# Moving one copy of the rotary query split from VectorE to ScalarE, at 14 places of an attention kernel

## What is computed

```python
q_C = (c_Q @ W_UQ.T)            # 16 heads, 128 wide
q_R = rope(c_Q @ W_QR.T, pos)   # 16 heads, 64 wide: the rotary queries
q = concatenate([q_C, q_R]); k = concatenate([k_C, rope(x @ W_KR.T, pos)])
scores = clip(einsum('bhqd,bhkd->bhqk', q, k), -80, 80)
weights = softmax(where(causal, scores, -inf) / sqrt(192))
attn = einsum('bhqk,bhkd->bhqd', weights, v)
out = x + (attn @ W_O.T) * silu(ffn(x))
```

## Time and profile before

| what | us |
|---|---|
| median of 3 runs | 1460.11 |
| lowest, highest | 1458.19, 1461.9 |
| the profiled execution's own time | 1460.29 |
| its span, first to last instruction | 1458.8 |
| TensorE busy | 1383.0 |
| VectorE busy | 1155.1 |
| ScalarE busy | 769.5 |
| GpSimd busy | 111.4 |

### The profile page before, as it was taken

One profiled execution on the slowest core, in us unless ns is written; L12 is line 12 of the kernel. 1 busy time (PEld: TensorE's weight loads), 2 busy tenths in 40 slices (PEclk: granted clock), 3 DMA queues, 4 the chain that ended last, 5 costly groups with the idle time before them and its releaser, 6 DMA issues. The chain is left out here.

```text
span 1458.8 us, 27828 instructions
## 1 busy us (share of the span) xinstructions
PE 1383.0 (95%) x9808; PEld 1120.5 (77%) x9808; DVE 1155.1 (79%) x1336; ACT 769.5 (53%) x840; POOL 111.4 (8%) x150
## 2 busy tenths in 40 slices
PE   4999689999999999999999999999999899599998
PEld 4888567777778888887878888887888788278887
DVE  4666388898898898989888898899788699476664
ACT  3322356656665656565666656656656566332221
POOL 0000111101001000000010000000100000112121
PEclk9999899999999999999999999999999999899999
DMA  6423565545425424333142421421422511345652
GB/s 253 144 73 101 161 201 160 164 136 145 126 84 153 116 93 99 109 101 108 54 147 62 126 83 54 126 83 54 131 58 61 217 57 58 117 125 158 183 171 87
DMA packets 111949, 172.77 MB, mean 118 GB/s; under 512 B 9224, under 2 KB 68904, under 8 KB 109096
## 3 DMA queue, kind: packets, MB, share of 16 engines
q1 hardware_dynamic: 97528, 111.10, 24.7%
q0 software_dynamic: 13552, 59.60, 14.0%
q10 hardware_dynamic: 832, 1.57, 0.5%
HBM read 123.75 MB, written 48.50 MB: 118 GB/s over the span
## 5 line engine op out<-in xcount | busy, mean ns | idle before, releaser
L1093 ACT CAST prob_h<-prob 128x1024 fp32r<-128x1024 f32 (+1 forms) x288 | 289.8, 1006 | 245.8 <-DVE prob L1174 195.7
L1087 ACT ACTIVATE prob<-score_ps 128x1024 f32<-128x1024 f32 (+1 forms) x288 | 281.9, 979 | 170.5 <-PE score_ps L946 117.2
L1192 DVE TENSOR_TENSOR prob_l<-prob,prob_h 128x1024 fp32r<-128x1024 f32 (+1 forms) x288 | 336.0, 1167 | 39.7 <-ACT prob_h L1093 38.3
L946 PE MATMUL score_ps<-q_h,key_slot 64*128 64x512 f32 x1792 | 357.8, 393 | 7.9 <-DMA key_slot<-keys 7.8
L968 PE MATMUL out_ps<-prob_h,value_slot 64*128 64x512 f32 (+1 forms) x1792 | 340.4, 377 | 5.5 <-DVE prob_l L1192 5.0
L1187 DVE TENSOR_TENSOR total<-total,prob 128x1024 f32<-128x1024 f32 (+1 forms) x256 | 294.9, 1152 | 0.0
L1174 DVE TENSOR_SCALAR prob<-prob 128x1024 f32<-128x1024 f32 x224 | 155.1, 692 | 80.3 <-ACT prob L1087 80.1
L946 PEld LDWEIGHTS score_ps<-q_h,key_slot 64*128 64x128 f32 x1792 | 170.9, 185 | 48.2 <-DMA key_slot<-keys 7.3
L968 PEld LDWEIGHTS out_ps<-prob_h,value_slot 64*128 64x128 f32 x1792 | 170.7, 185 | 48.1 <-DVE prob_l L1192 12.2
L946 PE MATMUL score_ps<-q_l,key_slot 64*128 64x512 f32 x896 | 177.7, 391 | 0.0
L946 PE MATMUL score_ps<-rot_hh,key_slot 64*128 64x512 f32 x896 | 177.5, 390 | 0.0
(11 more groups left out here) (192 smaller groups left out, 1975.5 us busy)
## 6 DMA issues: line engine op xcount, KB each, us to landing
key_slot<-keys SPq DMA_DIRECT2D x144, 256.0 KB, 2.7
value_slot<-values SPq DMA_DIRECT2D x144, 128.0 KB, 2.0
rows<-heads_rows SPq DMA_DIRECT2D x32, 512.0 KB, 5.7
rot_hh<-turned POOLq DMA_DIRECT2D x30, 512.0 KB, 6.2
heads_rows<-head_rows POOLq DMA_DIRECT2D x15, 1024.0 KB, 9.5
turned<-rot_hl POOLq DMA_DIRECT2D x14, 1024.0 KB, 5.1
rot_l<-turned POOLq DMA_DIRECT2D x30, 256.0 KB, 7.6
wo<-in_w_o POOLq DMA_DIRECT2D x1, 4096.0 KB, 13.3
```

The source lines that it names most:

```text
L946: mm = pe.matmul(score_ps[:, half, c * 512:(c + 1) * 512], keys_of[ROWS[r], :], moving[par][ROWS[r], half * HW + c * 512:half * HW + (c + ...
L1087: nc.scalar.activation(prob[half][:, 0:width], score_ps[:, half, 0:width], ACT.Exp, scale=QK_SCALE).then_inc(exp_done, 1)
L1093: nc.scalar.copy(prob_h[half][:, 0:width], prob[half][:, 0:width]).then_inc(high_done, 1)
L1192: nc.vector.tensor_tensor(p_l, p, p_h, ALU.subtract).then_inc(split, 1)
```

## The change

In the program of ScalarE, behind its second `high` of a LATE pair of couple 0 and of a FULL pair k = 1 of the other couples, stands a copy of `rot_f` into the high half of `rot_hl`, with the waits that VectorE's copy had. VectorE keeps only the difference.

```diff
@@ ScalarE: def pair(t, unit, k, slot, kind, prev) @@
                     for half in range(2):
                         exponential(half)
                         high(half)
+                    first_couple = isinstance(unit.couple, int) and unit.couple == 0
+                    if unit.has_second and (kind == LATE and first_couple or
+                                            kind == FULL and isinstance(k, int) and k == 1):
+                        since(act, passed, 16 * n)
+                        act.wait_ge(r_step, 4 * n + 2)
+                        nc.scalar.copy(rot_hl[:, 0, :, :], rot_f[:, :, :]).then_inc(r_step, 1)
                     return
@@ VectorE: def split_turned(n) @@
-                since(dve, passed, 16 * n)
-                dve.wait_ge(r_step, 4 * n + 2)
-                nc.vector.tensor_copy(rot_hl[:, 0, :, :], rot_f[:, :, :]).then_inc(r_step, 1)
                 dve.wait_ge(r_step, 4 * n + 3)
                 nc.vector.tensor_tensor(rot_hl[:, 1, :, :], rot_f[:, :, :], rot_hl[:, 0, :, :],
                                         ALU.subtract).then_inc(r_step, 1)
```

## The result

| | us |
|---|---|
| before, median of 11 runs | 1458.69 |
| changed, median of 11 runs | 1453.53 |
| lowest and highest, before / changed | 1457.36, 1461.9 / 1449.74, 1456.6 |
| ratio, with its 95% interval | 0.9956 [0.9947, 0.9965] |
| span of the profiled execution, before / changed | 1458.8 / 1452.1 |

A forecast was written before the change was run, and what follows sets the result against it. TensorE was taken to set the time, stalled ten times by VectorE's copy and difference. -7.15 (units 4 to 13) - 0.9 (units 2 and 3) + 0.65 (units 0 and 1) = -7.4 us, giving 1452.7 us; range 1450.5 to 1457.5.

The forecast's parts named there:

- What bounds the kernel: TensorE sets the time; ten waits for `prob_l` behind VectorE's copy and difference in units 4 to 13 lose 7.6 us.
- The size of the stalls: Units 4 to 13: each place gets back the smaller of its loss and 0.72 us, 7.15 us in all.
- the bracket of idle time (0.45): Listed idle time at a TensorE stall, counted from the modelled end of the matmul before; distances of starts gave 0.71 lost.
- The cover on ScalarE: At the 12 FULL places the copy costs nothing: 0.2 us ahead of need, next exponential 0.4 us or more to spare.
- Couple 0: Units 0 and 1: nothing covers the copy, the difference starts 0.35 and 0.3 us later; cost +0.65 us, bounds 0.3 and 2.1.
- Couple 1: Units 2 and 3: TensorE's stalls for `total` and the turned products at the next CORNER end; 0.9 us gained, bounds 0.4 and 1.2.
- Rival 1: Another wait, a later `prob_l` or a key tile, comes due at the ten places; half of each stall stays: 1456.8, chance 0.12.
- Rival 2: ScalarE's copy starts late and is hidden nowhere; 0.35 us at each of 14 places, +4.9 us: 1465.0, chance 0.05.
- The rule against the change: Skill advice to use VectorE, not ScalarE, for simple elementwise work; by it alone the copy's move would give the slower 1465.0.

## Why the prediction was right, and where not

**What bounds the kernel: right.** The ten waits for `prob_l` were one event, they belong to the block of copy and difference on VectorE, and they are gone. Lengthening the block by 0.60 us lengthened each stall by 0.60.

**The size of the stalls: right.** 7.15 us were forecast for couples 2 to 6, and units 4 to 13 are 7.0 us shorter. That the bracket of idle time (0.45) is not the loss (0.71), and that the starts have to be compared, made the difference between 5.0 and 7.15. It could be checked so closely because units 5 to 13 repeat to 0.1 us between profiles of the kernel before.

**The cover on ScalarE: right.** The copy was worked out to start 0.95 us behind the high half and the exponential 1.90; they do (516.60, 517.55, 518.50). The clip came 0.72 us earlier against its low half, as said. The 0.4 us to spare were 0.45.

**Couple 0: the local delay is right, its price in time is not shown.** +0.35 and +0.3 were forecast, and the difference starts 0.35 and 0.33 us later in both kernels that have this part. What it costs disappears in the scatter of loads and of the clock: unit 0 takes 25.7 to 26.35 us where VectorE does the copy and 26.0 to 26.7 where ScalarE does, unit 1 differs by 1.6 us between profiles of before, and units 0 and 1 together came out at +1.3 in the change instead of +0.65.

**Couple 1: the gain is there, in one of its two stalls.** -0.9 was forecast for what follows units 2 and 3, and these take 1.4 us less in the mean, more than forecast. TensorE's summing matmul behind unit 2 came 0.56, 1.01 and 1.02 us behind the matmul ahead of it in the profiles of before (0.56 is the one in the earlier trace rows) and comes at 0.32 in all four of the change; behind unit 3 it is 0.51, 0.48 and 0.47 against 0.32 to 0.34. The stall for the turned products did not end at unit 3's CORNER as forecast: 0.56 us before, 0.48 to 0.58 after. Waits for key tiles of 1.0 and 1.4 us stand in units 2 and 3 in the change's first profile and of 0.6 and 1.1 in that of before, so the size is not a clean number.

**The step that was missing**: the key tile behind the load of `wo`. Rival 1 named key tiles, but at the ten places, where no wait for one is listed in any of these profiles. In the rest of units 4 to 13 its waits for them add up to 1.5 to 2.3 us in the profiles of before and to 1.6 to 4.8 in those of the change, and yet these units are 7.0 us shorter. The loss came at the end: +1.9 us in units 14 and 15, which the forecast took as moving rigidly with the rest. So `attend` is 5.3 us shorter in the profiles and not 7.4. The timed runs say 6.0 to 6.7 in four comparisons. The profiles come near to that only with the 1.0 us that stands ahead of `attend`; whether the timed runs hold such a part too isn't shown, and if they do, the total agrees better than the forecast earned. Why that key tile comes later in the kernels with both parts stays open.

**Rival 2's price** does not follow from its own condition. It says that the gain ends when the copy is 0.92 us late (0.72 + 0.2; its 0.95 is a slip) and then charges 0.35 at every place. With the second copy on ScalarE it is about that late, and the clip starts 3.04 us behind the low half instead of 3.00 before: 0.04 a place, and the time of before, not 1465.

**The rule against the change** (the Trainium skill, ScalarE: Activation LUTs, Rules for kernel authors) names `relu`, `max`, `min`, `add` and `mul` as work for VectorE; to apply it to a copy, as the prediction did, goes one step further. The trace agrees on the instruction, 1.05 us against 0.69. As a decision it would have been wrong at the ten places, where VectorE was waited for and ScalarE was not. In couple 0, where nothing covered the copy, its price is what the trace shows: the difference starts 0.35 us later.

## What to carry to other kernels

Look for the one stall that repeats with a period of the program, and count it: ten waits for ten units said more than an engine at 79%. Measure it by the starts of the waiting engine's instructions, and price the cover of the engine that takes the work by two numbers, how long until its result is needed and how long until its next instruction is; here 0.2 and 0.45 us, so that one copy was free and a second took all the gain back. Where the gain is a few us, compare the stretches that repeat between profiles to a tenth, and not the whole time, which moves by two us and more by itself (1457.36 to 1461.9 for the kernel before).

## What the runs showed of the hardware

- A matmul stream that resumes after a stall for its operand loses about 0.10 us more than the gap: the next start is 0.34 us behind instead of 0.23 (528.43 and 528.77; at all ten stalls of the three profiles of before, and not here in the change, 523.16 and 523.39). The same 0.34 stands at a few of the ten places in the change, where TensorE starts 0.05 to 0.06 us behind the end of `prob_l` and no wait is listed.
- Two casts on ScalarE, 1.05 us each, start 0.95 us apart; two on VectorE, 0.69 each, start 0.60 apart where the second waits for nothing (527.59 and 528.19); VectorE's difference, which waits for the copy, starts 0.72 behind it (523.48 and 524.20).
- The wait for a 256 KB key tile behind a 4 MB load differs by kernel (4.3 to 5.0 us in eight profiles, 5.7 to 6.4 in six) and repeats within each to 0.7 us, although the two loads are issued at the same distance. What decides it stays open.
- At the same place of the program, after a wait of 1.9 to 3.1 us for a gather, TensorE's clock was at 1.2 GHz in some executions and at 2.4 GHz in others of the same kernel (0.51 in one of before, 1.00 in two), which goes with about 2 us of unit 1. It was not found what tips it.
